# Attention with exact row maxima: next phase's row scores in six of eight key steps, maxima turned one step earlier

## What is computed

```python
xf  = gn(x).reshape(b, c, 1024)                       # block 1; block 3 is the same after a layer norm
q, k, v = split(W_qkv @ xf + b_qkv)                   # 8 heads of 32 channels
scores = einsum('bthe,bThe->bhtT', q, k) / sqrt(32)   # 1024 x 1024 for each head
attn = softmax(scores, axis=-1)                       # exp(s - max of the row) / sum of the row
out = einsum('bhtT,bThe->bthe', attn, v)
x = x + proj(out)
```

## Time and profile before

| | us |
|---|---|
| median of three runs | 5773.23 |
| lowest and highest of them | 5773.15, 5781.61 |
| the profiled execution, its own time | 5776.78 |
| its span, first to last instruction | 5775.1 |
| mean granted clock of TensorE | 0.838 of full speed |

### The profile page before, as it was taken

One profiled execution on the slowest core, in us unless ns is written; L12 is line 12 of the kernel. 1 busy time (PEld: TensorE's weight loads), 2 busy tenths in 40 slices (PEclk: granted clock), 3 DMA queues, 4 the chain that ended last, 5 costly groups with the idle time before them and its releaser, 6 DMA issues.

```text
span 5775.1 us, 54320 instructions
## 1 busy us (share of the span) xinstructions
PE 4286.4 (74%) x16298; PEld 1857.3 (32%) x16298; DVE 3890.3 (67%) x4825; ACT 2116.3 (37%) x2575; POOL 2221.7 (38%) x721
## 2 busy tenths in 40 slices
PE   4677966788668886588855888558785587855878
PEld 2233422333223332233322433224332243322433
DVE  7763778647786477864777646876468764687646
ACT  3233442334323343233532335323353242532425
POOL 4541435414354044540445404454044440444404
PEclk7689977899778997689976999769997699976999
DMA  0020100201002100021000210002200022000120
GB/s 34 0 52 13 32 8 0 52 22 24 8 8 45 29 17 8 8 45 36 10 8 8 45 43 2 8 8 45 44 1 8 8 45 44 1 8 5 40 44 8
DMA packets 58928, 126.15 MB, mean 22 GB/s; under 512 B 14713, under 2 KB 16889, under 8 KB 58370
## 3 DMA queue, kind: packets, MB, share of 16 engines
q1 hardware_dynamic: 58626, 122.39, 9.1%
HBM read 12.23 MB, written 8.39 MB: 4 GB/s over the span
## 4 chain that ended last, share of the span: by engine, by line
PE 47%; DVE 26%; issue 11%; POOL 5%; ACT 4%; SPq 4%; DMA 2%; DVEq 0%; POOLq 0%; ACTq 0%
PE PS L1246 8%; PE PS L1288 8%; PE PS L1336 7%; PE PS L1080 6%; DVE mx L947 6%; POOL work L399 4%; PE PS L1370 4%; PE PS L1139 3%; PE PS L1180 3%; SPq L284 2%; DVE mboth L954 2%; SPq L293 2%; DVE small L714 2%; PE PS L1297 2%; DVE work L841 2%
## 5 line engine op out<-in xcount | busy, mean ns | idle before, releaser
L947 DVE TENSOR_REDUCE mx<-PS 128x1 f32<-128x512 f32 x2048 | 1336.3, 686 | 407.2 <-PE PS L1246 402.5
L617 ACT ACTIVATE PT<-PS 128x1024 f32<-128x1024 f32 x1024 | 1013.7, 1022 | 709.5 <-PE PS L1336 702.3
L1246 PE MATMUL PS<-KS,QS 96*128 96x512 f32 x2048 | 896.7, 481 | 191.7 <-DMA KS<-piece 85.5
L423 POOL TENSOR_TENSOR piece<-PT 128x2048 f32<-128x2048 f32 x48 | 219.8, 4580 | 2011.6 <-ACT PT L617 2011.6
L423 POOL TENSOR_TENSOR piece<-piece,PT 128x2048 f32<-128x2048 f32 x192 | 877.7, 4571 | 62.0 <-ACT PT L617 39.3
L399 POOL TENSOR_TENSOR work<-work,Crep 128x1024 f32<-128x1024 f32 x256 | 616.7, 2410 | 443.9 <-DVE work L839 244.6
L1336 PE MATMUL PS<-QS,KS 98*128 98x512 f32 x2048 | 692.0, 433 | 45.4 <-DMA QS<-nm 28.9
L1246 PEld LDWEIGHTS PS<-KS,QS 96*128 96x128 f32 x2048 | 378.2, 197 | 814.1 <-DVE mx L947 592.8
L1288 PE MATMUL PS<-PT,Vt 128*32 128x512 f32 x4096 | 564.3, 624 | 7.9 <-ACT PT L617 7.9
L1180 PE MATMUL PS<-dstk,sel 128*128 128x512 f32 (+1 forms) x640 | 318.1, 571 | 325.9 <-DVE work L841 133.4
L1180 PE MATMUL PS<-ustk,sel 128*128 128x512 f32 (+1 forms) x640 | 332.5, 593 | 283.7 <-DVE work L824 153.6
(11 more groups left out here) (212 smaller groups left out, 5553.1 us busy)
## 6 DMA issues: line engine op xcount, KB each, us to landing
QS<-piece SPq DMA_DIRECT2D x384, 128.0 KB, 2.4
KS<-piece SPq DMA_DIRECT2D x384, 128.0 KB, 2.4
xin<-x SPq DMA_DIRECT2D x8, 1024.0 KB
out<-xr SPq DMA_DIRECT2D x8, 1024.0 KB, 5.9
W<-wpack SPq DMA_DIRECT2D x2, 1024.0 KB
QS<-nm SPq DMA_DIRECT2D x128, 8.0 KB, 1.9
W<-wpack SPq DMA_DIRECT2D x1, 576.0 KB
W<-wpack SPq DMA_DIRECT2D x2, 256.0 KB
```

Source lines behind the costliest of these rows:

```text
L423: pool.tensor_tensor(total, first, PT[:, i % 3, :, :], ALU.add).then_inc(sum_pool.sem, 1)
L617: act.activation(PT[:, i % 3, 2 * pr:2 * pr + 2, :], PS[:, 2 + 2 * pr:4 + 2 * pr, :], ACT.Exp, scale=SCALE).then_inc(p_sb.sem, 1)
L947: dve.tensor_reduce(mx[:, cc, at:at + 1], PS[:, row_slot(n, cc), :], AX.X, ALU.max).then_inc(r_max.sem, 1)
L1246: pe.matmul(PS[:, row_slot(n, cc), :], QS[0:kd, c, h, q * P:q * P + P], KS[0:kd, h, cc * N:cc * N + N], start=True, stop=True).then_inc(r_ ...
```

## The change

Two constants. The number of halves in a phase stays 32 and no instruction is added or removed. Steps 0 to 5 now have 6, 5, 5, 5, 6, 5 halves, and steps 6 and 7 have none. The transposition, ScalarE's and VectorE's parts of the negated maxima, and with them the two DMAs, belong to step 6.

```diff
@@ -49,8 +49,8 @@
 PHASES = GROUPS * NC
-HALF_ROWS = (5, 4, 4, 4, 5, 5, 5, 0)
-TURN_AT = 7
+HALF_ROWS = (6, 5, 5, 5, 6, 5, 0, 0)
+TURN_AT = 6
 AHEAD = 3
 NORM_AT = 4
```

## The result

The changed kernel takes 5915.32 us (median of four runs, 5892.93 to 5931.42) against 5775.53 us for the kernel before (5773.15 to 5781.61): ratio 1.0238, 95% interval 1.0195 to 1.028, 2.4% slower. The forecast was 5841 us in a range of 5795 to 5900. The direction was right, the size was not, and the runs of the changed kernel scatter over 38 us where those of before scatter over 8.

A forecast was written before the change was run, and what follows sets the result against it. TensorE was taken to bound the kernel, with waits for a bank's maximum and for `mboth` at the turn. Terms of 2.09 + 0.67 + 0.71 - 2.06 = +1.41 us over 48 phases gave +68 us, 5841 us, range 5795 to 5900.

The forecast's parts named there:

- The intervals: TensorE times between starts of successive key steps' eight value matmuls, written v(k) for step k; net +1.41 us a phase.
- v(3) to v(4): From step 3's value matmuls to step 4's: a sixth half waits one VectorE pitch more, +0.67 us.
- v(7) to v(0): From step 7's value matmuls to the next step 0's: the sixth half in step 0 adds 0.71 us.
- The idle time ahead of the seventh half: In step 0, TensorE waits about 0.9 us because the seventh half needs the maximum of the fifth.
- The sum: Per phase 2.09 + 0.67 + 0.71 - 2.06 = +1.41 us; 48 times that, +68 us, gives 5841 us.
- The price of a moved half: Steps 1 to 3 going from four to five halves: 4.11 us instead of 3.41 each, +2.09 us together.
- The rival in which the latency spreads out: Early steps: a moved half costs only its own 0.24 to 0.34 us; 5756 us, chance 0.07.
- The turn: In step 6, `mboth` waits for GpSimd's sum of step 5; TensorE idles 0.84 us where it idled 1.03.
- the rival with the missed gap: At the turn, GpSimd's next sum goes first and `mboth` waits for it too; about 6065 us, chance 0.02.
- The prediction's gain of 2.06: Emptied steps 5 to 7: 2.06 us saved a phase, of about 2.9 without the sum in the way.
- The DMAs: SyncE's two DMAs go out a step earlier, ending a 0.54 us wait at the fourth phase, worth nothing.
- The clock: Rival: idle time in steps 6 and 7 halves TensorE's clock, 82 us more, 5923 us; chance 0.10.

The follow-up runs named there:

- step0_filled: Changed kernel plus three unused matmuls ahead of the seventh half, at step 1 of the second and third phases; 5832.98 us.
- steps123: Kernel before with three halves moved from step 6 to steps 1, 2 and 3, turn left in step 7; 5766.02 us.
- step0_kept: Changed kernel, but step 0 keeps its five halves and step 5 takes the sixth, turn in step 6; 5807.61 us.
- rows_moved_turn7: Changed kernel's halves, but with the turn left in step 7; 5829.7 us.
- the four filled or padded ones: Changed halves plus unused matmuls: three at the turn (5933 us) or in step 0 (5833); five at the turn left in step 7 (5885) or ending step 3 (5920).
- step0_alone: Kernel before with only one half moved, from step 6 to step 0, turn in step 7; 5904.61 us.
- turn_filled: Changed kernel plus three unused matmuls at each turn, ahead of the wait for `mboth`; 5933.02 us.
- spread_join: Kernel before with `mboth` as a reduction and, in steps 4 and 6, one half between the second pair's two scores; 5716.5 us.

## Why the prediction was right, and where it was wrong

**The intervals.** Each was right to within 0.07 us: steps 1 to 3 at 4.11, v(3) to v(4) 4.72 (4.78 forecast), v(5) at 4.01 (4.00), the transposition at 5.83 (5.84), v(6) at 7.04 (7.06), v(7) at 8.67 (8.70), v(7) to v(0) 9.14 (8.43 + 0.71). `mboth` took 1.499 us (about 1.5). The idle time ahead of the seventh half is 0.75 (0.9). The phase at full clock is 34.9 us, 1.3 more than before (1.41 forecast).

**The sum.** `step0_filled`, with this schedule and no fall behind step 0, takes 5833 us where the sum said 5841. That nearness is in part luck. In the profiled executions its second and third phases grew by 42 us, as forecast (45). But its first phases, from the first transposition to v(7), grew by 47 us where the prediction priced them like the others at 23: they start at a granted clock of 0.50, before and after, and the fuller step 0 is paid there at that clock (52 us in the changed kernel). Its fourth phases, from the third v(7) on, came out 31 us shorter, where the sum had nothing; without that the time would be some 5864.

**The price of a moved half.** Away from those starts, the latency of the cluster and not TensorE's own 0.24 to 0.34 us is what a half costs: `steps123` shows three times 0.7. The rival in which the latency spreads out has fallen.

**The turn.** `mboth` is held to the end of whichever sum runs: 2.13, 1.50, 0.82 (`step0_kept`), 2.80 and 0.175 us in five schedules, and 0.19 in the three kernels that make it a reduction. In the changed kernel, `rows_moved_turn7` and the four filled or padded ones the next sum was due right behind, and it got in between the two in all 277 cases; the rival with the missed gap has fallen. In the kernel before, `step0_kept` and `step0_alone` no sum was due yet, so that there was no gap to miss. The prediction's gain of 2.06 was right (10.77 less 8.68). Its statement that a turn in step 6 meets another sum holds, and `rows_moved_turn7` adds what it left out: with the rows moved, leaving the turn in step 7 would have been the better half of the change, by 0.9 us a phase.

**The DMAs** were worth nothing, as forecast: the waits for them at line 1336 fell from 48 to 32, and the fourth phase did not get shorter (16.4 us from v(0) to v(7) in the mean, 16.5 before).

**The clock is the step that failed.** I gave it 0.10, on the ground that a stretch with 2.36 of 3.40 us busy had kept its clock. That reading was no evidence: the stretch in the changed kernel ahead of the fall has 2.46 of 3.40, more than that, and `rows_moved_turn7` has a stretch with the same 2.46 and no fall:

```profile
641.70:645.10 3.40, 2.46 (x8) 1.28 (x8) 3.36 (x6) 2.49 (x4) 0.00 (x0) 1.00 0.00 0
```

The rival's price came out (82 us forecast, 82 measured between the changed kernel and `step0_filled`), but by luck: it had 1.7 us in each of 48 phases, and the measured difference is made of 15 falls behind step 0 and of the fourth phases. Its place was wrong: not steps 6 and 7, where `turn_filled` took away most of the turn's idle time without effect and `step0_filled` left all of it and had no fall, but step 0, for which the prediction had written down a new wait of 0.9 us and priced it only as time. It was wrong in the distribution too: not a bit of half clock in every phase, but none in 17 of the 32 second and third phases, 3.4 us in ten and 30.7 us in five. These five, 11 us each, make 55 of the 68 us by which the second and third phases are longer than those of `step0_filled`. The scatter of 38 us between runs would fit a varying number of such long stretches; only one execution of the four was profiled. Why a fall lasts 3.4 us at one time and 30.7 at another stays open. The forecast with the clock's 82 us would have been 5923, and the range, which stopped at 5900, had been closed against just this case.

The Trainium skill, page "TensorE: Matmul & The Clock Gate", section "A second HAM failure mode: psum-queue depth-cycling", names such a case: TensorE idling briefly and often between groups of matmuls, so that the clock goes back and forth. By the trace I set it aside, since the phases of before had idle times of the same size. The runs agree with the page: 15 falls in 32 phases, with no idle time above 0.76 us near any of them.

**Sign.** Slower was forecast at 0.88, and three mechanisms add up to it: five clusters (+3.5 us a phase), a turn that meets another sum and a new wait for the exponentials (a gain of 2.1 us instead of the 3.0 of `rows_moved_turn7`), and a clock that falls behind step 0 (68 us in the profiled execution, very unevenly). The fuller start of the first phases adds to it.

## What to carry to other kernels

Price a moved instruction by the latency of the buffer it reuses at its new place, not by its duration; and where two engines share a port, ask which instruction of the other is running at the new time. A wait of under a microsecond on TensorE can cost more in clock than in time: when a change adds one, compare the granted clock by stretches before and after, and try it with unused matmuls in the gap. A run that keeps its clock may do so by timing alone: look whether the idle place was met by one of the moments at which the clock changes. A join of two small operands next to a busy GpSimd is better written as an operation with one SBUF input, here worth 1.1%.

## What was not expected of the hardware

- The clock fell to half with no single idle time above 0.76 us near it, and once low it stayed there for 30.7 us while TensorE was 42.94 of 45.80 us busy. In that state a step of five halves takes 6.73 us, not 4.11.
- The same instructions with the same waits keep the clock or lose it depending on when they run: adding five matmuls elsewhere brought the falls back in one kernel (0 to 72 us inside) and reduced them in the other (188 to 82). What decides is whether one of the evenly spaced moments of clock change meets the end of step 0: 66 of 66 such phases fell, 0 of 126 others.
- The two-input join, held by a running GpSimd sum for up to 1.50 us, got in ahead of the next sum each of the 277 times that one was due, although the two sums are only 0.16 us apart.
- The start of the fourth phase loses its half-clock stretch (75 us in all) when a 1.03 us wait some 6 us earlier is removed. How these two are linked stays open: `spread_join`, without that wait either, has the stretch again.
